# Two weight-preparation loops with per-slot load gates, and a layer norm transposed by token block

## The reference

```
q, k, v = x @ wq.T, x @ wk.T, x @ wv.T        # 16 heads of 128
q = (q @ fq1.T + b) * (q @ fq2.T + b)         # k the same with fk1, fk2
# linear attention, causal: o = q (sum of earlier k^T v) + masked (q k^T) v
attn = rmsnorm(o) * norm_w @ wo.T
# ffn: the weight is made from 4 "bit" planes of 2048 x 2048 x 4 float32
soft   = sigmoid(pweight) - sigmoid(nweight)              # [out, in, 4]
weight = einsum('oin,n->oi', soft, exps * sigmoid(mask)) * scale
ffn = x @ weight.T + bias
```

## Time and profile before

| | us |
|---|---|
| timed runs (2): median, lowest, highest | 11272.22, 11231.3, 11313.14 |
| the profiled execution: time, span | 10852.45, 10850.8 |
| spans of the 8 cores in it | 10741.9 to 10850.8 |
| busy: TensorE, VectorE, ScalarE, GpSimd | 6589.5, 2303.8, 1236.9, 189.4 |
| stage 38 to 628: wq, wk, wv, wo | 590 |
| stage 628 to 1770: FFN weight | 1142 |

### The profile page before, as it was taken

One profiled execution on the slowest core, in us unless ns is written; L12 is line 12 of the kernel. 1 busy time (PEld: TensorE's weight loads), 2 busy tenths in 40 slices (PEclk: granted clock), 3 DMA queues, 4 the chain that ended last, 5 costly groups with the idle time before them and its releaser, 6 DMA issues.

```text
span 10850.8 us, 85077 instructions; the slowest of 8 cores (10741.9 to 10850.8 us)
## 1 busy us (share of the span) xinstructions
PE 6589.5 (61%) x31754; PEld 3238.8 (30%) x31754; DVE 2303.8 (21%) x3794; ACT 1236.9 (11%) x1981; POOL 189.4 (2%) x170
## 2 busy tenths in 40 slices
PE   3310001666656666577776577776577777577767
PEld 3310001222222222233343233333234333244322
DVE  2334443001010010111211222211222211222211
ACT  2222221000000000011110011100011100011100
POOL 2210000000000000000000000000000000000000
PEclk6555555998989989888888788888888888788888
DMA  7843333332323323232311333211323211323212
GB/s 199 225 159 139 133 126 99 84 86 75 87 78 83 84 74 86 82 69 72 77 54 59 94 70 70 66 59 57 95 67 70 64 62 58 91 66 72 55 62 76
DMA packets 1260013, 945.63 MB, mean 87 GB/s; under 512 B 826715, under 2 KB 1220699, under 8 KB 1241179
## 3 DMA queue, kind: packets, MB, share of 16 engines
q1 hardware_dynamic: 1234364, 839.51, 27.7%
q0 software_dynamic: 25248, 100.68, 3.4%
HBM read 839.38 MB, written 100.67 MB: 87 GB/s over the span
## 4 chain that ended last, share of the span: by engine, by line
PE 44%; DMA 32%; DVE 12%; ACT 5%; issue 4%; DVEq 2%; SPq 1%; ACTq 0%; POOLq 0%
PE pb L181 15%; PE pb L183 13%; PE pb L182 13%; DMA wsv<-sc_wv 13%; DMA wsk<-sc_wk 4%; DMA wst<-sc_wf 3%; DMA wst<-sc_wo 3%; DVE x_t L355 2%; PE pb L268 2%; DMA wbuf<-pw 2%; DMA wbuf<-nw 2%; DVE x_t L344 2%; PE pb L478 1%; ACT wbuf L351 1%; ACT wbuf L335 1%
## 5 line engine op out<-in xcount | busy, mean ns | idle before, releaser
L181 PE MATMUL pb<-wsv,lnf_hi 128*128 128x512 bf16 x2048 | 813.2, 397 | 965.6 <-DMA wsv<-sc_wv 875.4
L181 PE MATMUL pb<-lnf_hi,wsk 128*128 128x512 bf16 x2048 | 803.6, 392 | 172.0 <-DMA wsk<-sc_wk 165.9
L182 PE MATMUL pb<-wsv,lnf_hi 128*128 128x512 bf16 x2048 | 815.3, 398 | 0.0
L183 PE MATMUL pb<-wsv,lnf_lo 128*128 128x512 bf16 x2048 | 815.2, 398 | 0.0
L182 PE MATMUL pb<-lnf_lo,wsk 128*128 128x512 bf16 x2048 | 802.4, 392 | 0.0
L183 PE MATMUL pb<-lnf_hi,wsk 128*128 128x512 bf16 x2048 | 801.2, 391 | 0.0
L268 PE MATMUL pb<-id128f_s,x_t 128*128 128x128 f32 x256 | 57.1, 416 | 1083.0 <-DVEq L358 1083.0
L181 PEld LDWEIGHTS pb<-wsv,lnf_hi 128*128 128x128 bf16 x2048 | 204.4, 100 | 1549.8 <-issue 1432.7
L478 PE MATMUL pb<-id128f_s,wbuf 128*128 128x128 f32 x768 | 189.2, 424 | 680.8 <-DVEq L468 617.7
L195 DVE SCALAR_TENSOR_TENSOR v_lo<-pb,v_hi 128x512 bf16<-128x512 f32 x128 | 82.7, 687 | 2442.5 <-ACT v_hi L189 2442.2
L181 PE MATMUL pb<-wst,o_hi 128*128 128x512 bf16 x1024 | 394.7, 385 | 113.6 <-DMA wst<-sc_wo 76.1
(11 more groups left out here) (176 smaller groups left out, 9344.2 us busy)
## 6 DMA issues: line engine op xcount, KB each, us to landing
wsv<-sc_wv SPq DMA_DIRECT2D x1024, 256.0 KB, 3.1
wsk<-sc_wk SPq DMA_DIRECT2D x256, 512.0 KB, 6.0
wbuf<-pw SPq DMA_DIRECT2D x16, 4096.0 KB, 13.9
wbuf<-nw SPq DMA_DIRECT2D x16, 4096.0 KB, 12.3
wsq<-sc_wq SPq DMA_DIRECT2D x128, 512.0 KB, 6.1
wst<-sc_wo SPq DMA_DIRECT2D x256, 256.0 KB, 3.0
wst<-sc_wf SPq DMA_DIRECT2D x256, 256.0 KB, 3.0
wbuf<-wq SPq DMA_DIRECT2D x16, 1024.0 KB, 5.2
```

The costliest lines, as they stand in the source:

```text
L181: T.matmul(out, lT_hi, r_hi, start=start, stop=False, tile_position=tp)
L182: T.matmul(out, lT_hi, r_lo, start=False, stop=False, tile_position=tp)
L183: return T.matmul(out, lT_lo, r_hi, start=False, stop=stop, tile_position=tp)
```

## The change

Three edits.

1. *wq to wo.* The load into a quarter of `wbuf` waits for the transposes that last read that quarter (`tr_ev[buf]`), not for those of the chunk before. The two quarters count on two semaphores, `s_ld` and `s_x`.
2. *FFN weight.* `wbuf` is two slots of 4096 columns. A block is four steps: first half of `pw`, second half of `pw`, first and second half of `nw`, in slots 0, 1, 0, 1, each with its own load of 2 MB, sigmoid of 4096 columns and four VectorE operations of 1024 columns into its half of `pacc`. A slot is loaded again as soon as its own operations are done, so the first two loads of a block can be issued during the block before. The first loads wait for TensorE's count after the small matmul L319.
3. *`emit_ln`.* The addition of epsilon moves into the statistics loop. Normalisation sets an event per token block. The transposes go by token block (outer) and group of four column groups (inner): a bank then holds four column groups of one token block, and cast and subtraction write four pieces of 128 elements each, a stride of 512 apart. The wait on both engines' latest counts stays where it is.

```diff
--- before.py
+++ after.py
@@ -293,16 +293,19 @@
                 stg_gate[buf] = ev_w
                 return (evt[-1])
 
-            prev_tr = ev_tr_prev
+            tr_ev = [ev_tr_prev, ev_tr_prev]
+            ldsem = [s_ld, s_x]
+            gidx = 0
             for which in ("q", "k", "v", "o"):
                 wd = w_d[which]
                 for oc in range(NIC):
-                    buf = oc % 2
+                    buf = gidx % 2
                     region = wbuf[:, buf * D:(buf + 1) * D]
-                    ev_l = load(region,
-                                wd[oc * 128:(oc + 1) * 128, :], s_ld, ev=prev_tr)
+                    ev_l = load(region, wd[oc * 128:(oc + 1) * 128, :],
+                                ldsem[buf], ev=tr_ev[buf])
                     wait(T, ev_l)
-                    prev_tr = prep_weight_chunk(region, which, oc)
+                    tr_ev[buf] = prep_weight_chunk(region, which, oc)
+                    gidx += 1
 
             ev1 = load_ser(row4[:], maskw_d.rearrange("(a b) -> a b", a=1))
             ev2 = load_ser(row4b[:], exps_d.rearrange("(a b) -> a b", a=1))
@@ -325,40 +328,55 @@
             ev_cc = sV.inc(V.drain())
 
             pacc = x_t[:, 0:D]
-            ev_acc_prev = prev_tr
+            ev_acc_prev = tr_ev[0]
             ev_tr_pacc = None
+            slot_gate = [(sT, sT.n), (sT, sT.n)]
+            slot_sem = [s_ld, s_x]
             for oc in range(NIC):
-                buf = oc % 2
-                ev_lp = load(wbuf[:, 0:4 * D], pw_d[oc * 128:(oc + 1) * 128, :],
-                             s_ld, ev=ev_acc_prev)
-                wait(S, ev_lp)
-                ev_sp = sS.inc(S.activation(wbuf[:, 0:4 * D], wbuf[:, 0:4 * D],
-                                            AF.Sigmoid, bias=0.0, scale=1.0))
-                sp4 = wbuf[:, 0:4 * D].rearrange("p (i n) -> p n i", n=4)
-                wait(V, ev_sp)
-                wait(V, ev_cc)
-                wait(V, ev_tr_pacc)
-                V.tensor_scalar(pacc, sp4[:, 0, :], cc[:, 0:1], None, OP.mult)
-                V.drain()
-                for n in range(1, 4):
-                    V.scalar_tensor_tensor(pacc, sp4[:, n, :], cc[:, n:n + 1],
-                                           pacc, OP.mult, OP.add)
-                    V.drain()
-                ev_pc = sV.inc(V.drain())
-                ev_ln_ = load(wbuf[:, 0:4 * D], nw_d[oc * 128:(oc + 1) * 128, :],
-                              s_ld, ev=ev_pc)
-                wait(S, ev_ln_)
-                ev_sn = sS.inc(S.activation(wbuf[:, 0:4 * D], wbuf[:, 0:4 * D],
-                                            AF.Sigmoid, bias=0.0, scale=1.0))
-                wait(V, ev_sn)
-                for n in range(4):
-                    V.scalar_tensor_tensor(pacc, sp4[:, n, :], ncc[:, n:n + 1],
-                                           pacc, OP.mult, OP.add)
-                    V.drain()
-                ev_acc_prev = sV.inc(V.drain())
-                wait(T, ev_acc_prev)
+                rows = slice(oc * 128, (oc + 1) * 128)
+                slots = (wbuf[:, 0:4 * D // 2], wbuf[:, 4 * D // 2:4 * D])
+                ev_ld = [None, None, None, None]
+                for j, (wd_, half) in enumerate(((pw_d, 0), (pw_d, 1),
+                                                 (nw_d, 0), (nw_d, 1))):
+                    pass
+                ev_ld[0] = load(slots[0], pw_d[rows, 0:4096], slot_sem[0],
+                                ev=slot_gate[0])
+                ev_ld[1] = load(slots[1], pw_d[rows, 4096:8192], slot_sem[1],
+                                ev=slot_gate[1])
+                ev_chain = [None, None, None, None]
+                for j in range(4):
+                    half = j % 2
+                    neg = j >= 2
+                    slot = slots[half]
+                    if oc == 0 and j == 0:
+                        wait(V, ev_cc)
+                    wait(S, ev_ld[j])
+                    ev_sg = sS.inc(S.activation(slot, slot, AF.Sigmoid,
+                                                bias=0.0, scale=1.0))
+                    sp4 = slot.rearrange("p (i n) -> p n i", n=4)
+                    co = ncc if neg else cc
+                    dst = pacc[:, half * 1024:(half + 1) * 1024]
+                    wait(V, ev_sg)
+                    if not neg:
+                        wait(V, ev_tr_pacc)
+                        V.tensor_scalar(dst, sp4[:, 0, :], co[:, 0:1],
+                                        None, OP.mult)
+                        V.drain()
+                        nstart = 1
+                    else:
+                        nstart = 0
+                    for n in range(nstart, 4):
+                        V.scalar_tensor_tensor(dst, sp4[:, n, :], co[:, n:n + 1],
+                                               dst, OP.mult, OP.add)
+                        V.drain()
+                    ev_chain[j] = sV.inc(V.drain())
+                    slot_gate[half] = ev_chain[j]
+                    if j < 2:
+                        ev_ld[j + 2] = load(slot, nw_d[rows, half * 4096:
+                                                       (half + 1) * 4096],
+                                            slot_sem[half], ev=ev_chain[j])
+                wait(T, ev_chain[2]); wait(T, ev_chain[3])
                 ev_tr_pacc = prep_weight_chunk(pacc, "f", oc)
-
             ev_pb_ = load_ser(b16r.rearrange("p (ic n) -> p ic n", n=4),
                               pbias_d.rearrange("(ic p) n -> p ic n", p=128))
             ev_nb_ = load_ser(b16br.rearrange("p (ic n) -> p ic n", n=4),
@@ -445,7 +463,6 @@
                     V.drain()
                     V.bn_aggr(stat[:, tb * 2:tb * 2 + 2], mv[:])
                     V.drain()
-                for tb in range(TB):
                     V.tensor_scalar(rstd4[:, tb:tb + 1],
                                     stat[:, tb * 2 + 1:tb * 2 + 2],
                                     EPS, None, OP.add)
@@ -457,34 +474,43 @@
                 V.reciprocal(rstd4[:], rstd4[:])
                 V.drain()
                 wait(V, st8["wbuf_free"])
-                if taps:
-                    wait(V, s_tap.now())
+                ev_ap = [None] * TB
                 for tb in range(TB):
                     V.tensor_scalar(wbuf[:, tb * D:(tb + 1) * D],
                                     src[:, tb * D:(tb + 1) * D],
                                     stat[:, tb * 2:tb * 2 + 1],
                                     rstd4[:, tb:tb + 1], OP.subtract, OP.mult)
-                    V.drain()
-                ev_ap = sV.inc(V.drain())
-                wait(T, ev_ap)
+                    ev_ap[tb] = sV.inc(V.drain())
                 wait(T, st8["lnf_free"])
                 wait(T, sS.now()); wait(T, sV.now())
                 ev_lnf = None
-                for ic in range(NIC):
-                    bank = pb[4 + (ic % 2)]
-                    wait(T, ln_psum_gate[ic % 2])
-                    e = None
-                    for tb in range(TB):
-                        e = T.transpose(bank[:, tb * 128:(tb + 1) * 128],
-                                        wbuf[:, tb * D + ic * 128:
-                                             tb * D + (ic + 1) * 128],
-                                        id128f[:])
-                    evt = sT.inc(e)
-                    _, ev_lnf = split(bank[:, 0:512],
-                                      lnf_hi[:, ic * TILE:(ic + 1) * TILE],
-                                      lnf_lo[:, ic * TILE:(ic + 1) * TILE],
-                                      wait_s=evt)
-                    ln_psum_gate[ic % 2] = ev_lnf
+                for tb in range(TB):
+                    wait(T, ev_ap[tb])
+                    for grp in range(4):
+                        bank = pb[4 + (grp % 2)]
+                        wait(T, ln_psum_gate[grp % 2])
+                        e = None
+                        for j in range(4):
+                            ic = grp * 4 + j
+                            e = T.transpose(bank[:, j * 128:(j + 1) * 128],
+                                            wbuf[:, tb * D + ic * 128:
+                                                 tb * D + (ic + 1) * 128],
+                                            id128f[:])
+                        evt = sT.inc(e)
+                        hi4 = lnf_hi.rearrange("p (ic tt) -> p ic tt", ic=NIC)[
+                            :, grp * 4:(grp + 1) * 4, tb * 128:(tb + 1) * 128]
+                        lo4 = lnf_lo.rearrange("p (ic tt) -> p ic tt", ic=NIC)[
+                            :, grp * 4:(grp + 1) * 4, tb * 128:(tb + 1) * 128]
+                        wait(S, evt)
+                        eh = sS.inc(S.copy(hi4, bank[:, 0:512].rearrange(
+                            "p (j c) -> p j c", j=4)))
+                        wait(V, eh)
+                        il = V.scalar_tensor_tensor(
+                            lo4, bank[:, 0:512].rearrange("p (j c) -> p j c",
```

(4 more changed lines are left out.)

## The result

| us | before | changed |
|---|---|---|
| median of the timed runs | 11169.87 (10 runs) | 10545.66 (11 runs) |
| lowest, highest | 10855.75, 11313.14 | 10338.12, 10882.29 |
| ratio, 95% interval | | 0.9525, 0.9468 to 0.9582 |

The change takes 4.75% off by this ratio, which uses only the executions in which no half of the chip ran at a clearly lower granted clock; the medians of all executions are 5.6% apart. The two lowest times are 518 us apart.

What follows compares the result with a forecast made beforehand. Both weight loops were taken as bound by a serial chain of loads and compute, not by an engine. FFN loop 431 us plus first loop 132, layer norm zero, made 563 off 11272: 10709 us, range 10210 to 10900.

Steps and rivals of the forecast that it cites:

- the clock that the prediction wrote down: FFN loop: step-by-step timing of one block from the last chain's end; 43.7 us where it took 70.9.
- the fixed cost of an operation: FFN loop: extra time of each 1024-column VectorE operation, taken as 0.08 us, between nothing and 0.16.
- three candidates: First loop, what limits a chunk next: chain inside a turn 5.3 us, staging buffer 6.0 or 7.6, DMA engines 6.9 or 7.5.
- the DMA engines (6.9 and 7.5): First loop: moving a chunk's loads and stores takes 6.9 us by throughput, 7.5 by packet times; 7.2 taken.
- The staging buffer: First loop: a chunk's cast waits for the stores of two chunks back; 6.0 us a turn, or 7.6.
- The 50 us: Layer norm: gain in all if the wait on VectorE's latest count were gone, 4.2 us hidden 12 times.
- Rival 1: First loop gains nothing, a load wait being exchanged for a store wait; time 10841 us, chance 0.13.
- Rival 2: First loop falls to 5.3 us a chunk; saves 253 + 431 us, time 10588, chance 0.10.
- the chain: First loop: transposes to last split inside one turn, which the next transposes wait for; 5.3 us at best.
- Rival 3: FFN loop: VectorE stands still during all four sigmoids, block 58 us; saves 334 us, time 10938, chance 0.10.
- Rival 4: First loop: prefetched loads crowd out stores, 11.5 us a chunk, loss 138; chance 0.05 shared with an FFN overlap collapse.
- the band of 10640 to 10820: Whole kernel: the forecast's own range, from a block of 42.5 to 46 us and chunk of 6.3 to 8.2.

Runs made afterwards that it cites:

- e7: Changed kernel with a third 2 MB slot in the FFN loop; FFN block 41.0 us, against 44.8 in the changed kernel.
- e9: e7 with the next block's first sigmoid issued ahead of the casts in ScalarE's queue; FFN block 38.1 us, against 41.0 in e7.
- e8: Kernel before with each VectorE operation of the FFN loop cut into two of 1024 columns; FFN block 73.0 us, against 70.8 before.
- e6: Changed kernel with four staging buffers in place of two; mean chunk of the first loop 7.23 us, against 7.84 in the changed kernel.
- e3: Kernel before with only the layer norm edit; ratio to before 1.0005, layer norm 28.65 us against 28.76.
- e4: Changed kernel with TensorE waiting for VectorE's count taken ahead of the four normalisations; layer norm 26.53 us against 28.58, ratio to before 0.949.
- e1: Kernel before with only the first edit, the load gates for wq to wo; mean chunk 7.99 us against 9.31, ratio to before 0.986.

## Why the prediction was right, and where it was off

*FFN blocks: the mechanism and the size hold.* Predicted 43.7 us, measured 44.8. Each step of the clock that the prediction wrote down is in the trace: a reload of slot 0 that lands in 7.7 us (median of the 32 loads of nw, predicted 7.7), a sigmoid of 3.62 (3.6), idle stretches of 2.90 and 4.30 us (about 3 and 4.2), VectorE as the engine that bounds the loop. e7 and e9 remove the stretches one by one. What was mis-sized is the fixed cost of an operation. I added 0.08 us to each of the 16 operations of a block, which makes 1.3 us, or 0.16 for each of the 8 that the change adds. The prediction's later sentence that puts its own figure at 0.64 us a block, and its gain at 10 us too much by the Trainium skill's rule, misreads this: it counts 8 operations where its clock has 16. Measured is 0.21 us for an added operation by itself and 0.27 with its drain, 2.2 us a block (e8). The difference of 0.9 us is most of the 1.1 that were missing, and the 0.01 us that each operation takes longer in the changed kernel than in e8 makes 0.2 more. In the block shown the four half chains take 32.3 us, where my clock has 31.0; the rest of it agrees to 0.1. The Trainium skill's rule on the fixed latency of SBUF-source operations (VectorE: DVE Perf Modes, TRN2 errata), about 150 cycles or 0.156 us, is what my clock already held, and the measurement lies above it. 15 blocks gave 390 us instead of 408, the first block 24 instead of 23 (21 over the eight cores).

*First loop: right in kind, mis-sized by 40 us.* Predicted 7.2 us a chunk, measured 7.84; 92 us instead of 132. The prediction weighed three candidates for what is late next, and its 7.2 lies with the DMA engines (6.9 and 7.5), which did not come last. The staging buffer did: ScalarE waits for stores, and e6 takes 0.6 us off by freeing it. I had worked this candidate out for the landing of 6.4 us, which made 6.0 us a turn, and for 9.5, which made 7.6. Once loads were always in flight the second store of a chunk, the one that the buffer waits for, landed in 9.9 us, and the same formula then gives (4.0 + 1.65 + 9.9)/2 = 7.8. So the term that failed is the landing time of a store: in this loop full DMA engines also stretched the wait beside them. The 7.23 us of e6 at a DMA share near 1 are close to my 7.2, but this owes something to luck, since my two workings had given 6.9 and 7.5. The DMA share that I had expected above 0.95 was 0.94.

*Layer norm: nothing, as predicted.* e3 shows it, and e4 shows that the cause is the wait on the latest count. The 50 us which I had given for that wait's removal were wrong: e4 finds 25 in the layer norms, because VectorE's queue holds the splits behind all four normalisations.

*The rivals.* Rival 1 (no gain in the first loop) is refuted by e1, although its premise holds: the DMA engines are nearly full. Rival 2 (down to the chain) is refuted by e6, which frees the buffers and stays at 7.2. Its figure of 344 GB/s for mixed traffic came from 4 us of a turn in which loads outweighed stores; over whole stretches e6 moves 264 to 303. Rival 3 (VectorE standing still beside ScalarE) is refuted by the changed kernel's own trace: the half chain from 1018.47, with a sigmoid beside it, takes 8.42 us, and the one from 1027.13, with none, 8.34; e8 says the same. Rival 4 was there in small: stores land later, which costs 0.6 us a turn, and the loop still gains.

*The sum.* 563 us predicted, 508 measured in the trace and 518 between the lowest times. The absolute time, 10709 predicted against 10546, is off by 163 us, three times as much as the gain (55 or 45). It lies below the band of 10640 to 10820 to which the prediction gave 0.62, although block and chunk both lie in the bands behind it. The base of 11272.22 was the median of two runs, and ten give 11169.87; and the medians are 624 us apart, the lowest times 518. The doubt about the base, not that about the change, had to set the range's lower end, and did.

## What to carry to other kernels

In a stage in which every compute engine is busy less than half of the time, look for a chain: write down one turn on a clock and edit it. In the FFN loop the idle stretches of the new turn came out to 0.1 us. Look at the DMA share as well: at 0.81 before the change, it left the first loop little room. For each prefetch, work out the next gate with the landing times of the loaded state, not with today's. A finer wait does nothing while a coarser one on the same engine stands in front of it, and once it is gone, look at the queue of the next engine.

## What the runs showed of the hardware that I had not expected

- The scalar_tensor_tensor of the FFN loop (float32, one input with a stride of 4) costs 0.21 us more in two pieces of 1024 columns than in one of 2048, more than the 0.16 us that a whole copy of 4 columns out of PSUM takes in the trace.
- The two stores of a chunk are issued 1.15 us apart, but in the changed kernel the second takes 3.2 us longer to land than the first (9.9 against 6.7), where before it was 1.1 us longer.
- A DMA share near 1 is no fixed throughput. In e6 a share of 0.96 went with 303 GB/s from 38 to 270 us, and one of 0.99 with 264 GB/s from 270 to 520.
- Stores of wv and wo have rows of 256 bytes as those of wq and wk have, but 8 KB apart in HBM where those of wq and wk are 512 bytes apart; with four buffers their chunks take 7.84 and 7.62 us against 6.72 and 6.90 (over the eight cores 7.9 against 6.7 and 6.9). That the scatter is the cause was not tried.
